# Masked attention over 4096 nodes, eight heads: one visit of TensorE to the values in each step instead of two

## The reference

```python
h = jnp.maximum(_layernorm(x, axis=-1), 0.0)
adj = jnp.maximum(adjacency_matrix, eye)
q, k, v = (jnp.einsum('nd,hdk->hnk', h, W) for W in (Wqs, Wks, Wvs))
scores = jnp.einsum('hqk,hmk->hqm', q, k) * kd ** (-0.5)
scores = scores + IDENTITY_BIAS * eye - MASK_VAL * (1.0 - adj)
att = jax.nn.softmax(scores, axis=-1)
x = x + jnp.einsum('hqm,hmk,hko->qo', att, v, Wo)
```

## Time and profile before

| | |
|---|---|
| median of 3 runs | 2651.34 us |
| profiled execution | 2648.64 us |
| its span, first to last instruction | 2647.1 us |
| PE, DVE, ACT, POOL busy | 98%, 85%, 70%, 48% |
| granted TensorE clock | 0.998 of full speed |

### The profile page before, as it was taken

The page is one execution under the profiler, slowest core; times in us unless marked ns, Lnnn a source line. Parts: engine busy times, 40 slices in busy tenths (PEclk is TensorE's granted clock), DMA queues, the critical chain, the costliest instruction groups (busy, mean ns, idle before and its releaser), DMA issues.

```text
span 2647.1 us, 58489 instructions
## 1 busy us (share of the span) xinstructions
PE 2597.6 (98%) x17344; PEld 1897.9 (72%) x17344; DVE 2254.0 (85%) x3833; ACT 1844.7 (70%) x3041; POOL 1281.6 (48%) x2424
## 2 busy tenths in 40 slices
PE   8999999999999999999999999999999999999997
PEld 5777777777777777777767777777777777777775
DVE  8888888888888888888858888888888888888885
ACT  5677676776767767777747677777767777776764
POOL 3355655556566555665403444434343444434343
PEclk9999999999999999999999999999999999999999
DMA  7467777677778767787645556666555666655563
GB/s 187 125 166 169 182 177 181 171 166 173 174 177 192 171 167 166 172 181 176 162 137 126 138 144 152 165 145 161 144 138 145 153 161 147 162 141 140 144 145 105
DMA packets 268608, 419.06 MB, mean 158 GB/s; under 512 B 100544, under 2 KB 121536, under 8 KB 268544
## 3 DMA queue, kind: packets, MB, share of 16 engines
q1 hardware_dynamic: 178784, 231.24, 34.3%
q0 software_dynamic: 89760, 187.05, 30.8%
HBM read 136.84 MB, written 46.27 MB: 69 GB/s over the span
## 4 chain that ended last, share of the span: by engine, by line
PE 85%; SPq 5%; DMA 4%; DVE 3%; issue 2%; POOL 0%; ACT 0%; DVEq 0%; POOLq 0%; ACTq 0%
PE psS L511 31%; PE psO L548 16%; PE psT L524 15%; PE psO L534 15%; SPq L301 5%; DMA S<-S 3%; PE psS L181 2%; DVE S L777 2%; PE psP L496 2%; PE psP L165 2%; PE psP L484 1%; DVE S L798 1%; PE psO L484 1%; DMA rden_scratch<-rden 0%; POOL S L362 0%
## 5 line engine op out<-in xcount | busy, mean ns | idle before, releaser
L362 POOL DMA_DIRECT2D S<-S x2048 | 1005.6, 499 | 1098.2 <-DVE S L798 1047.3
L777 DVE CUSTOM_DVE_ANT_0 S<-psS,B 128x1024 f32<-128x1024 f32 x1024 | 1227.5, 1218 | 217.8 <-PE psS L511 149.2
L662 ACT ACTIVATE S<-S,negm 128x1024 f32<-128x1024 f32 (+1 forms) x768 | 1095.9, 1428 | 43.9 <-DVE negm L784 43.5
L669 ACT ACTIVATE PT<-psT 128x512 f32<-128x512 f32 x1024 | 594.8, 595 | 254.0 <-PE psT L524 235.3
L511 PE MATMUL psS<-K,QH 128*128 128x512 f32 x2048 | 724.8, 435 | 16.9 <-DVE mx L777 16.4
L511 PE MATMUL psS<-K,QL 128*128 128x512 f32 x2048 | 640.5, 394 | 0.0
L798 DVE STREAM_TRANSPOSE S<-S 128x2048 f32<-128x2048 f32 x256 | 590.4, 2306 | 38.7 <-PE psO L548 35.2
L524 PEld LDWEIGHTS psT<-ident,S 128*128 128x128 f32 x4096 | 480.5, 140 | 185.9 <-issue 73.1
L524 PE MATMUL psT<-ident,S 128*128 128x128 f32 x4096 | 606.6, 276 | 2.9 <-ACT PT L669 2.9
L534 PE MATMUL psO<-PT,V 128*64 128x256 f32 x4096 | 492.1, 382 | 0.0
L548 PE MATMUL psO<-S,V 128*64 128x256 f32 x4096 | 470.3, 382 | 2.4 <-DMA S<-S 2.4
(11 more groups left out here) (51 smaller groups left out, 968.4 us busy)
## 6 DMA issues: line engine op xcount, KB each, us to landing
S<-S SPq DMA_DIRECT2D x2048, 64.0 KB, 3.0
S<-S POOLq DMA_DIRECT2D x2048, 64.0 KB, 2.8
B<-in_adj POOLq DMA_DIRECT2D x128, 256.0 KB, 6.8
bias_scratch<-B SPq DMA_DIRECT2D x64, 512.0 KB, 3.8
B<-bias_scratch SPq DMA_DIRECT2D x128, 256.0 KB, 4.3
hq<-hT_scratch SPq DMA_DIRECT2D x32, 256.0 KB, 4.8
RB<-rden_scratch SPq DMA_DIRECT2D x128, 64.0 KB, 3.4
S<-in_x SPq DMA_DIRECT2D x8, 512.0 KB, 4.6
```

The costliest lines, as they stand in the source:

```text
L362: pool.dma_start(dst, src).then_inc(late_sent[q][half], 16)
L662: nc.scalar.activation(part, part, ACT.Exp, bias=negm[:, h % 2, q:q + 1], accum_out=sums[:, h % 2, q, e:e + 1]).then_inc(probs_ready, 1)
L669: nc.scalar.activation(PT[:, s % RING, :], psT[s % 2][:, :], ACT.Copy).then_inc(pt_act, 1)
L777: nc.vector.tensor_tensor_reduce(out=part, in0=psS[j % 2][:, :], in1=B[:, q, k * SLOT:(k + 1) * SLOT], scale=SCALE, scalar=LOWEST, op0=ALU ...
```

## The change

The ring of 4 places stays for transposed slots 0 to 3. Slots 4 to 7 are written over score columns of the same head that have been transposed already (`PT_of`). With that, PE does all 8 transposes first, then visits the values once (slots 0 to 3, late tiles, slots 4 to 7), and makes score slots 0 and 1 of the head after next behind the visit. ACT takes the exponentials in a new order (`EXP_ORDER`: the third piece of both row halves last), the third piece of the first half behind the copy of the output. On DVE the row's maximum of the first half comes behind mask 4, `sum_halves` and `denominators` behind mask 5, the low parts of the queries behind the first late transpose, and masks 0 and 1 of the head after next behind the second.

```diff
+EXP_ORDER = [(0, 0), (0, 1), (1, 0), (1, 1), (0, 2), (1, 2)]
+def exps_done(q, e):
+    return EXP_ORDER.index((q, e)) + 1
...
+    def PT_of(h, s):
+        if s < RING:
+            return PT[:, s, :]
+        first = (s - RING) * 2 * QW
+        return S[:, h % 2, 0, first:first + 2 * QW]
...
         def load_next_group(chunks):
-            pool.wait_ge(late_used, STEPS - 1)
+            pool.wait_ge(pt_free, STEPS * TS)
...
         def step(i, h, nxt, nxt2, prev):     # PE
-            for s in range(4):
+            transposes(i, h, 0)
+            transposes(i, h, 1)
+            if nxt:
+                scores(i1, h1, 2)
+            transposes(i, h, 2)
+            if nxt:
+                scores(i1, h1, 3)
...
+            if nxt2 and h % 2 == 0:
+                query(i2, h2, h2 == 0, isinstance(i, int) and i == 0 and h == 0)
+            for s in (3, 4):
                 transposes(i, h, s)
                 if nxt:
-                    scores(i1, h1, 2 + s)
...
+                    scores(i1, h1, s + 1)
+            transposes(i, h, 5)
+            for s in (6, 7):
+                transposes(i, h, s)
+                if nxt:
+                    scores(i1, h1, s)
...
             for s in range(4):
                 values(i, h, s)
-            for s in range(4, 6):
-                transposes(i, h, s)
-                if nxt:
-                    scores(i1, h1, 2 + s)
-            transposes(i, h, 6)
-            transposes(i, h, 7)
+            values_late(i, h, range(LATE))
+            for s in range(4, TS):
+                values(i, h, s)
             if nxt2:
                 scores(i2, h2, 0)
...
             if nxt2:
                 scores(i2, h2, 1)
-            values_late(i, h, range(LATE))
-            for s in range(4, TS):
-                values(i, h, s)
...
         def step(i, h, nxt, nxt2, prev):     # DVE
             if nxt:
                 mask(i1, h1, 2)
                 mask(i1, h1, 3)
+                mask(i1, h1, 4)
+                row_done(i1, h1, 0)
+                mask(i1, h1, 5)
             if prev:
                 sum_halves(*last_step(i, h))
+            denominators(i, h)
             if nxt:
-                mask(i1, h1, 4)
-                mask(i1, h1, 5)
+                mask(i1, h1, 6)
+                mask(i1, h1, 7)
+                row_done(i1, h1, 1)
+                transpose_late(i1, h1, 0, True)
             if nxt2 and h % 2 == 0:
                 query_lo(i2, h2, 0)
                 query_lo(i2, h2, 1)
-            denominators(i, h)
+            if nxt:
+                transpose_late(i1, h1, 1, True)
             if h % 2 and not (isinstance(i, int) and i == 0 and h == 1):
                 add_heads(*((i, 1) if h == 3 else (i - 1, 3)))
-            if nxt:
-                mask(i1, h1, 6)
-                mask(i1, h1, 7)
-            if nxt:
-                transpose_late(i1, h1, 0, True)
             if nxt2:
                 mask(i2, h2, 0)
                 mask(i2, h2, 1)
-            if nxt:
-                transpose_late(i1, h1, 1, True)
```

More of the change, by code:

```diff
@@ L68, in staged_in @@
     return divmod(j - SPT, HALVES)
[L71 to L75, removed]
 def wait_apart(engine, sem, value, passed):
@@ L268, in rows_again @@
             sp.wait_ge(late_used_before, STEPS)
-            sp.wait_ge(pt_free_before, RING + STEPS * TS)
+            sp.wait_ge(pt_free_before, TS + STEPS * TS)
             load_weights(Wv, wv, wv_in)
@@ L518, in transposes @@
                 if first_key == 2 * s * P:
-                    pe.wait_ge(probs_ready, count(i, h, QT * NE, NE + e + 1))
+                    pe.wait_ge(probs_ready, count(i, h, QT * NE, max(exps_done(q, e) for q in range(QT))))
             wait_taken(pe, i, h, s - 2)
@@ L534, in values @@
                 last = nc.tensor.matmul(psO[a * KD:(a + 1) * KD, 0:QW], V[:, 2 * s + a, h * KD:(h + 1) * KD],
-                                        PT[:, s % RING, a * QW:(a + 1) * QW], start=(s == 0), stop=(s == TS - 1))
+                                        PT_of(h, s)[:, a * QW:(a + 1) * QW], start=(s == 0), stop=(s == TS - 1))
             last.then_inc(pt_free, 1)
@@ L555, in step @@
             i2, h2 = (i, h + 2) if h + 2 < GROUP else (i + 1, h + 2 - GROUP)
-            for s in range(4):
+            transposes(i, h, 0)
[5 more added lines that the diff above has]
+                scores(i1, h1, 3)
+            if isinstance(i, int) and i == h == 0:
+                pe.wait_ge(v_dve, NC)
+            if nxt2 and h % 2 == 0:
+                query(i2, h2, h2 == 0, isinstance(i, int) and i == 0 and h == 0)
+            for s in (3, 4):
                 transposes(i, h, s)
                 if nxt:
-                    scores(i1, h1, 2 + s)
[L560 to L563, removed]
+                    scores(i1, h1, s + 1)
[4 more added lines that the diff above has]
+                    scores(i1, h1, s)
             if isinstance(i, int) and i == h == 0:
@@ L567, in step @@
                 values(i, h, s)
-            for s in range(4, 6):
-                transposes(i, h, s)
-                if nxt:
-                    scores(i1, h1, 2 + s)
-            transposes(i, h, 6)
-            transposes(i, h, 7)
+            if not nxt and g + 1 < GROUPS:
+                ahead[g + 1, "PE"](pe)
+            values_late(i, h, range(LATE))
+            for s in range(4, TS):
+                values(i, h, s)
             if nxt2:
@@ L581, in step @@
                 scores(i2, h2, 1)
-            if not nxt and g + 1 < GROUPS:
-                ahead[g + 1, "PE"](pe)
-            values_late(i, h, range(LATE))
-            for s in range(4, TS):
-                values(i, h, s)
-        pe.sem_inc(pt_free, RING)
+        pe.sem_inc(pt_free, TS)
         pe.sem_inc(projected, START)
@@ L667, in take_slot @@
             act.wait_ge(transposed, count(i, h, TS, s + 1))
-            act.wait_ge(pt_free, count(i, h, TS, ring_used(s)))
-            nc.scalar.activation(PT[:, s % RING, :], psT[s % 2][:, :], ACT.Copy).then_inc(pt_act, 1)
+            if s < RING:
+                act.wait_ge(pt_free, count(i, h, TS, s + 1))
+            nc.scalar.activation(PT_of(h, s), psT[s % 2][:, :], ACT.Copy).then_inc(pt_act, 1)
         def step(i, h, nxt, nxt2, prev):
@@ L677, in step @@
             take_slot(i, h, 2)
+            for s in range(3, 6):
+                take_slot(i, h, s)
+            if nxt:
+                exps(i1, h1, 0, 0)
             if nxt2 and h % 2 == 0:
                 query_hi(i2, h2)
-            take_slot(i, h, 3)
-            if nxt:
-                exps(i1, h1, 0, 0)
-            take_slot(i, h, 4)
-            if nxt:
-                exps(i1, h1, 0, 1)
-            take_slot(i, h, 5)
-            if nxt:
-                exps(i1, h1, 0, 2)
             take_slot(i, h, 6)
@@ L691, in step @@
             if nxt:
+                exps(i1, h1, 0, 1)
                 exps(i1, h1, 1, 0)
@@ L695, in step @@
                 ahead[g + 1, "ACT"](act)
-            act.wait_ge(pt_free, count(i, h, TS, TS + RING))
+            act.wait_ge(pt_free, count(i, h, TS, TS + TS))
             act.wait_ge(o_ready, count(i, h, 1, START))
             nc.scalar.activation(Oodd[:, :], psO[KD:2 * KD, 0:QW], ACT.Copy).then_inc(odd_copied, 1)
+            if nxt:
+                exps(i1, h1, 0, 2)
         if norm:
@@ L721, in scalar_program @@
         value_rows(EARLY + 2)
-        exps(0, 0, 0, 2)
         exps(0, 0, 1, 0)
         exps(0, 0, 1, 1)
+        exps(0, 0, 0, 2)
         value_rows(EARLY + 3)
@@ L779, in mask, with row_done @@
                                            accum_out=mx[:, h % 2, q, k:k + 1]).then_inc(slot_masked, 1)
[L780 to L785, removed]
+        def row_done(i, h, q):
+            dve.wait_ge(slot_masked, count(i, h, SLOTS, (q + 1) * SPT))
+            own = S[:, h % 2, q, bass.ds(i * QW + q * P, P)]
+            nc.vector.tensor_tensor(own, own, diag[:, :], ALU.add)
+            nc.vector.tensor_reduce(negm[:, h % 2, q:q + 1], mx[:, h % 2, q, :], AX_X, ALU.max,
+                                    negate=True).then_inc(row_ready, 1)
         def transpose_late(i, h, q, before):
-            dve.wait_ge(probs_ready, count(i, h, QT * NE, q * NE + 1))
+            dve.wait_ge(probs_ready, count(i, h, QT * NE, exps_done(q, 0)))
             if before:
@@ L893, in vector_program @@
             mask(0, 0, 2 * n + 1, first=True)
+            if n == 1:
+                row_done(0, 0, 0)
             if n == 2:
@@ L898, in vector_program @@
         mask(0, 0, 7, first=True)
+        row_done(0, 0, 1)
         mask(0, 1, 0)
```

## The result

The changed kernel takes 2766.83 us (median of 4 runs, 2759.87 to 2771.57) against 2651.64 for the kernel before (its median with a fourth run): a ratio of 1.044, 95% interval 1.0424 to 1.0456. The forecast was 2633, its range 2608 to 2669. The profiled execution took 2770.95 us.

What follows compares the result with a forecast made beforehand. TensorE, busy 98% of the span, was taken to bound the kernel. Terms of -36 (visit), +4 (DVE order), +9 and +3 (head 2's steps) and +2 (group boundary) sum to -18 us: 2633, range 2608 to 2669.

Steps and rivals of the forecast that it cites:

- The visit: On PE, one visit to the values instead of two saves 0.28 us a step, -36 us over 128 steps.
- rival D: At PE's weight loads, the pauses around a visit are all paid, 0.75 us a step: 2573; chance 0.06.
- rival C: On PE, only the entry to a visit is saved, 0.09 us a step, 12 us: 2657; chance 0.06.
- estimate of two drains: On PE, two tiling-mode switches, each draining about 128 cycles, would be 0.11 us, 14 us in all.
- The crowded step of the first group: Head 2's even step: late moves delay mask 7, PE stalls 1.8 us, 15 times: +9 us net.
- the second group's: Head 2's step there: moves behind bias loads waiting for mask 1, stall 0 to 0.8 us, 15 times: +3 us.
- The order on DVE: DVE's new order costs almost nothing: 0.06 us a pair of steps, +4 us, bounds 0 and 26.
- The low parts' cover: End of an even step: query's low parts done at 18.6, next score slot at 19.0; half a microsecond spare.
- The tight mask 0: Step after an even one: mask 0 ready 4.5 us after the late values, PE there after 4.6.
- the two stall terms: PE stalls in head 2's steps: +9 us in the first group, +3 in the second.
- Rival A: Mask 7 late in every even step, passed to PE through the query's low parts: +23 us, 2674; chance 0.20.
- What would show it: Signs: one weight-load pause, undisturbed steps of 18.1 and 19.8 us, head 2 stalls behind the values in the first group.

Runs made afterwards that it cites:

- two-visit experiment: Changed kernel with the addition early, but slot 7 transposed between the values of slots 0 to 3 and the late ones: 2656.36 us, ratio to before 1.003.
- the addition early: Changed kernel with the addition of heads back ahead of mask 6, behind the denominators: 2630.5 us, ratio to before 0.9936.
- best version: Changed kernel with the addition early and the next mask's two loads behind the second lot of head 2's moves: 2620.56 us, ratio to before 0.9889.

## Why the prediction was wrong

**The visit: right in kind, a little smaller than taken.** Forecast -36 us at 0.28 a step. The two-visit experiment gives 0.28 for an undisturbed step; against the kernel before, undisturbed steps give 19.27 - 19.05 = 0.22, -28. Neither the whole pauses of the loads (rival D, 0.75) nor the entry alone (rival C, 0.09) set the price. The estimate of two drains worked out from the Trainium skill's "TensorEngine Tiling (Array Packing)", Key Properties, and "TensorE: Matmul & The Clock Gate", Part 2 (0.11 us) is half of the smaller of these measured prices or less; the measurement decides.

**The crowded step of the first group and the second group's: the sizes fit, the places do not.** With the addition early, a pair stands 1.74 and 0.39 us above four undisturbed steps, against 1.12 and 0.17 before: +9 and +3 us over 15 pairs, the forecast's figures. In the first group the loads between the lots do hold the second lot of moves, as forecast: with them moved, 1.74 falls to 0.66. But the forecast let this delay reach PE through mask 7 and the query's low parts, at the score slot behind the values. It reaches PE mainly at the late values of head 2, which need the moves themselves. PE's waits there over the whole span, before, with the addition early, and in the best version:

```profile
PE psO L548 <- DMA S<-S: 2.4, 2, 1.3
PE psO L553 <- DMA S<-S: 17.5, 16, 2.1
PE psO L547 <- DMA S<-S: 3.8, 9, 1.2
```

The waits of the score slots for a mask fell meanwhile, from the 23.9 us of the earlier trace rows; with the addition early:

```profile
PEld psS L516 <- DVE mx L787: 12.3, 26, 1.7
```

In the second group one pair of the 14 makes most of the 0.39, with two stalls at the last two score slots of the step behind head 2's; no pair of the 14 waits at the score slot behind head 2's values, where the forecast put its stall. That both terms came out at their size is luck.

**The order on DVE: right in its sum, with one size wrong.** The low parts' cover was put at half a microsecond. Timelines of DVE and PE in the experiment with the addition early, where a step with an even head ends:

```profile
1078.71 1.71 DVE L770 TENSOR_TENSOR QL<-psP,QH 64x256 fp32r<-64x256 f32 x4
```

```profile
1080.07 0.73 PE L516 MATMUL psS<-K,QH 128*128 128x512 f32 x2
```

The score slot of the head after next starts 0.35 us before the low parts end (80.42): it needs only the first of their two pairs, so the cover was longer than forecast by the time of the second, about 0.9 us. The tight mask 0 cost nothing in undisturbed steps, also with the addition ahead of it: the interval 3 to 0 is 19.04 us with the addition late and 19.03 with it early, 0 for the forecast's +4. Behind head 2's crowded step of the first group it does cost: score slot 2 starts 1.17 us after the transposes ahead of it there (1084.08, after 1082.91), 0.79 in an undisturbed step, and mask 0 ends at 1084.02.

**What failed: the addition of heads.** The prediction carried it only as "(behind odd heads) the head addition", 0.69 us of DVE time ahead of mask 0. It did not ask who waits for it; nor does the text on the change name this move, which stands only in its diff. In the step of head 1 POOL's output store waits for it, and behind that store, in POOL's order, stand the load of the base rows and both lots of head 2's moves. The row "POOL out L369 <- DVE res" and the idle time ahead of it were in the trace of before; an addition moved behind the second late transpose was bound to delay that store, and with it the moves. Missing term: 15 pairs x (81.28 - 77.92 + 82.82 - 76.57) = 144 us, measured as 136. Without it, the sum came out right, 2630.5 against 2633, in part by luck: the visit gave 8 us less than taken, the order on DVE 4 us more, and the two stall terms fit in size only.

**Rival A** gave the right sign and for the wrong reason: the masks were late in one step of four, not in every even one, and the low parts had no share in it.

**What would show it: partly.** One pause instead of two appeared. Undisturbed steps shrank by 0.22 in the mean, but to 19.05 each, not to 18.1 and 19.8. The large stall stood elsewhere, at score slot 6 behind mask 4, released by a move.

## What to carry to other kernels

When an instruction moves, list who waits for its result, and for each of those, what is queued behind the waiter on its own engine. In this kernel a DVE instruction of 0.7 us held POOL's queue, and the next entries of that queue fed the engine that sets the time. Where a queue must hold both urgent moves and an output store, put the store behind the moves, so that its wait does not hold them (2640.25 us here, against 2766.83).

## What else the runs showed

A long stall cost more than itself here. Stretches of 2 us of the changed kernel around the stall (columns as in the earlier trace rows):

```profile
1570.00:1572.00 2.00, 0.00 (x0) 0.00 (x0) 0.00 (x0) 0.00 (x0) 0.00 (x0) 0.97 1.04 244
1572.00:1574.00 2.00, 0.00 (x0) 0.00 (x0) 0.77 (x1) 0.00 (x0) 0.00 (x0) 0.50 1.07 207
1574.00:1576.00 2.00, 1.48 (x4) 1.19 (x5) 0.90 (x5) 1.23 (x1) 0.00 (x0) 0.50 0.90 163
```

PE was idle from 1568.15 (1574.52 less the wait of 6.37). Meanwhile the granted clock went from full (2.4 GHz) to half (1.2 GHz), and PE came back at half. From score slot 6 to the values takes 1578.97 - 1574.52 = 4.45 us here against 1551.33 - 1548.86 = 2.47 in the undisturbed step. These 2 us are part of the 27.64, and the matmuls themselves show them: a QL pair takes 1.05 us, not 0.62.
